# Twelve value projections moved into the first half of an attention loop, on eight cores

## The reference

```
xn  = layernorm(x)
out = x + attention(xn) + ffn(xn)
```

## Time and profile before

| | |
|---|---|
| median of 3 runs | 786.75 us (786.33 to 796.28) |
| profiled execution | 791.31 us, span of its slowest core 789.8 us |
| spans of the cores | 770.2 to 789.8 us |
| TensorE busy | 697.0 us (88%) |
| VectorE, ScalarE busy | 376.4 us (48%), 287.2 us (36%) |
| DMA queue of POOL, queue of SP | 73.08 MB and 49.77 MB |

### The profile page before, as it was taken

One profiled execution on the slowest core, in us unless ns is written; L12 is line 12 of the kernel. 1 busy time (PEld: TensorE's weight loads), 2 busy tenths in 40 slices (PEclk: granted clock), 3 DMA queues, 4 the chain that ended last, 5 costly groups with the idle time before them and its releaser, 6 DMA issues.

```text
span 789.8 us, 11732 instructions; the slowest of 8 cores (770.2 to 789.8 us)
## 1 busy us (share of the span) xinstructions
PE 697.0 (88%) x4028; PEld 333.7 (42%) x4028; DVE 376.4 (48%) x658; ACT 287.2 (36%) x437; POOL 72.0 (9%) x111
## 2 busy tenths in 40 slices
PE   1667787396999998799999997999999999999998
PEld 1233343254545444344444443444444444444443
DVE  6597876268666667631132115552464443200341
ACT  2255575489676544215564553333200000000000
POOL 2001022011101100001111111010010000000000
PEclk9999999799999999999999999999999999999999
DMA  6668487959796945626656665352265454100552
GB/s 176 121 153 179 88 154 110 207 152 264 193 271 217 247 126 165 182 109 204 187 194 213 209 218 196 124 164 103 74 198 162 146 178 131 47 0 1 160 174 66
DMA packets 70329, 123.61 MB, mean 157 GB/s; under 512 B 34176, under 2 KB 39168, under 8 KB 70272
## 3 DMA queue, kind: packets, MB, share of 16 engines
q0 software_dynamic: 22880, 73.08, 32.3%
q1 hardware_dynamic: 47392, 49.77, 23.6%
HBM read 103.30 MB, written 16.78 MB: 152 GB/s over the span
## 4 chain that ended last, share of the span: by engine, by line
PE 69%; DMA 12%; issue 7%; DVE 5%; ACT 4%; SPq 2%; POOL 0%; DVEq 0%; ACTq 0%; POOLq 0%
PE pW L947 8%; PE pY L1042 7%; PE pST L1042 7%; PE pW L1042 7%; PE pSS L1042 7%; PE pSS L1019 6%; PE pST L1019 6%; PE pY L1019 5%; PE pW L1019 5%; DMA stg<-w1r 5%; PE pW L836 4%; PE pW L824 3%; DMA stg<-w2r 3%; DMA wv_sb<-wv 2%; ACT qf L735 2%
## 5 line engine op out<-in xcount | busy, mean ns | idle before, releaser
L753 ACT ACTIVATE stg<-stg 128x2048 f32<-128x2048 f32 x32 | 60.9, 1902 | 54.2 <-DMA stg<-w2r 44.8
L590 DVE TENSOR_SCALAR w1t<-stg,consts 128x2048 bf16<-128x2048 f32 x16 | 20.5, 1283 | 115.4 <-DMA stg<-w1r 95.8
L836 PE MATMUL pW<-wv_sb,xnT 128*128 128x512 bf16 x256 | 64.1, 396 | 5.0 <-DMA wv_sb<-wv 5.0
L1042 PE MATMUL pY<-w2t,hT 128*128 128x512 bf16 x256 | 66.0, 379 | 0.7 <-DVE osb L709 0.7
L1042 PE MATMUL pST<-w2t,hT 128*128 128x512 bf16 x256 | 66.1, 379 | 0.1
L1042 PE MATMUL pW<-w2t,hT 128*128 128x512 bf16 x256 | 66.1, 379 | 0.0
L1042 PE MATMUL pSS<-w2t,hT 128*128 128x512 bf16 x256 | 66.0, 379 | 0.0
L947 PE MATMUL pW<-wo_sb,yT 128*128 128x512 bf16 x256 | 60.4, 391 | 5.0 <-ACT qf L735 3.9
L1019 PE MATMUL pSS<-xnT,w1t 128*128 128x512 bf16 x272 | 61.5, 379 | 1.7 <-ACT hT L803 1.7
L1019 PE MATMUL pST<-xnT,w1t 128*128 128x512 bf16 x272 | 61.5, 379 | 0.0
L774 ACT ACTIVATE Am<-pSS,consts 128x1024 bf16<-128x1024 f32 x32 | 35.3, 1103 | 60.2 <-PE pSS L884 60.0
(11 more groups left out here) (140 smaller groups left out, 961.6 us busy)
## 6 DMA issues: line engine op xcount, KB each, us to landing
stg<-w1r POOLq DMA_DIRECT2D x32, 1024.0 KB, 7.2
stg<-w2r POOLq DMA_DIRECT2D x32, 1024.0 KB, 6.2
xr<-x SPq DMA_DIRECT2D x16, 512.0 KB, 5.1
xre<-x SPq DMA_DIRECT2D x16, 512.0 KB, 6.6
res_scr<-rst SPq DMA_DIRECT2D x16, 512.0 KB, 3.9
res<-res_scr SPq DMA_DIRECT2D x32, 256.0 KB, 4.1
out<-osb SPq DMA_DIRECT2D x32, 256.0 KB, 2.6
wv_sb<-wv POOLq DMA_DIRECT2D x2, 1024.0 KB, 15.9
```

The costliest lines, as they stand in the source:

```text
L590: e.tensor_single_scalar(dst, src, cc(col + 1), ALU.is_lt).then_inc(sTA, 1)
L753: e.activation(buf, buf, AF.Abs, accum_out=cc(col)).then_inc(done, 1)
L836: mm = e.matmul(work_bank(u), xnT[:, c, kd, :], wv[:, hf, kd, :], start=(kd == 0), stop=(kd == KD - 1))
L1042: return e.matmul(out_bank(n), hT[:, j, 128 * t:128 * t + 128], w2t[8 * dh + j // 4][:, j % 4, :], start=(j == 0), stop=(j == NJ - 1))
```

## The change

1. **Values early.** Values of chunks 16 to 27 are projected in i = 4 to 15 (`early_v(i)` = i+12), between the two halves of `spread_q`, emptied by ScalarE into a new tile `v2` at that place in its list, and no longer projected in i = 15 to 26. i = 27 to 30 still project theirs.
2. **Queries and keys in two steps.** `proj_qk("q")` stays at the end of i % 4 == 2; `proj_qk("k")` follows `scores` of i % 4 == 3, and VectorE empties it after the mask of that iteration.
3. **Weights earlier.** The second `wv` half is issued when 6 token tiles are normalised, ahead of the block copies of queries; `wo` (before: in the middle of the loop), `b2bc` and a1 0, a1 1 follow the first block copy. SP holds back the fifth token tile until the first `wv` has landed. `A1_SLOTS` are i = 8 to 23, `TH_SLOT` is 26.
4. **Ternary pieces.** t1 0 is made in halves at the ends of i = 28 and 29, t1 1 at i = 30 and 31, t1 2 after the loop, behind the last two `empty_wo`. t2 14 gets another place in SBUF and is made with t2 15 between the two halves of the output.
5. **Rows at the end.** `empty_wo` only copies; x is not read again in the loop. Each of the 32 output pieces reads its part of x (`xs`) beside `res`, and VectorE adds it in a further instruction (`dRX`).

```diff
+def early_v(i):
+    return i + 12 if 4 <= i < 16 else None
+def has_v(n):
+    return n < 16 or n >= 28
...
-Q_BEFORE = {("a1", 2): 3, ("a1", 6): 4, ("a1", 10): 5, ("a1", 14): 6, ("t1", 2): 7}
+Q_BEFORE = {("a1", 2): 2, ("a1", 4): 3, ("a1", 8): 4, ("a1", 12): 5, ("t1", 0): 6,
+            ("t1", 2): 7}
-A1_SLOTS = list(range(10, 26))
+A1_SLOTS = list(range(8, 24))
...
+            if t == 0:
+                e.wait_ge(dV[0], 16)
             if t + 4 < NT:
                 x_in(t + 4)
...
+            if n >= 2:
+                e.wait_ge(dRX, n - 1)
+            dXS.inc(e.dma_start(out=xs[:, n % 2, :],
+                                in_=x_d[t * 128:(t + 1) * 128,
+                                        dh * 512:(dh + 1) * 512]), n)
...
+        e.wait_ge(sXN, 6)
+        e.dma_start(out=wv[:, 1, :, :],
+                    in_=wv_d[1].rearrange("k p f -> p k f")).then_inc(dV[1], 16)
         q_block(e, 1, range(4, 8), dQP)
         e.dma_start(out=wqk[:, 1, :, :], in_=wqk_d[1]).then_inc(dQK[1], 16)
-        q_block(e, 2, range(4, 8), dQP)
-        e.dma_start(out=wv[:, 1, :, :], in_=wv_d[1].rearrange("k p f -> p k f")).then_inc(dV[1], 16)
+        e.dma_start(out=wo[:].rearrange("p k (h f) -> p (k h) f", h=2, f=512),
+                    in_=wo_d.rearrange("k h p f -> p (k h) f")).then_inc(dWO, 16)
...
-                e.tensor_tensor(rst[:, c % 2, sl], work_bank(UID[key]),
-                                xre[:, c % 2, sl], ALU.add).then_inc(dW, 1)
+                e.tensor_copy(rst[:, c % 2, dh * 512:dh * 512 + 512],
+                              work_bank(UID[key])).then_inc(dW, 1)
...
-            if i == 29:
-                ternary1(0)
-            if i == 30:
-                ternary1(1)
-            if i == 31:
-                ternary1(2)
+            if i in (28, 29):
+                ternary1(0, slice(1024 * (i - 28), 1024 * (i - 27)))
+            if i in (30, 31):
+                ternary1(1, slice(1024 * (i - 30), 1024 * (i - 29)))
...
+            dXS.wait_done(e, n)
+            e.wait_ge(dRB, n + 1)
+            e.tensor_tensor(res[:, n % 2, :], res[:, n % 2, :], xs[:, n % 2, :],
+                            ALU.add).then_inc(dRX, 1)
...
             scores(i)
+            if i % 4 == 3 and i // 4 < 7:
+                proj_qk("k", i // 4 + 1)
             if more:
-                proj_v(i + 1)
+                if has_v(i + 1):
+                    proj_v(i + 1)
                 spread_k(i + 1)
             y_before(i)
             if more:
                 spread_q(i + 1, 0)
+            if early_v(i) is not None:
+                proj_v(early_v(i))
             y_within(i)
```

More of the change, by code:

```diff
@@ L268, in ln_tiles, with values @@
         return ()
+    def values(n):
+        return v2[:, n - 16, :] if 16 <= n < 28 else v[:, n % 2, :]
     def q_block(e, B, heads, done):
@@ L355, in sync_stream @@
             dRS.wait_done(e, c)
+        e.wait_ge(pH, 2 * NJ)
         res_in(0)
@@ L585, in vec_stream, with ternary @@
         tern = [0]
-        def ternary(dst, key, col, done):
+        def ternary(dst, key, col, done, part=slice(0, 2048)):
             load_done(e, key)
-            src = stg[:, STG[LID[key]], :]
+            src = stg[:, STG[LID[key]], part]
+            dst = dst[:, part]
             e.tensor_single_scalar(dst, src, cc(col + 1), ALU.is_lt).then_inc(sTA, 1)
@@ L592, in ternary, with ternary1 @@
             e.wait_ge(sTA, tern[0])
-            e.scalar_tensor_tensor(dst, src, cc(col), dst, ALU.is_gt,
-                                   ALU.subtract).then_inc(done, 1)
-        def ternary1(u):
+            last = e.scalar_tensor_tensor(dst, src, cc(col), dst, ALU.is_gt,
+                                          ALU.subtract)
+            if part.stop == 2048:
+                last.then_inc(done, 1)
+        def ternary1(u, part=slice(0, 2048)):
             if u >= 3:
@@ L630, in vec_stream @@
                             ALU.mult).then_inc(dMK, 1)
+            if i % 4 == 3 and B < 7:
+                empty_qk("k", B + 1)
             for t in ln_tiles(i):
@@ L681, in vec_stream @@
         empty_wo(31)
-        for u in range(3, 12):
+        for u in range(2, 12):
             ternary1(u)
@@ L694, in vec_stream @@
         ternary1(15)
-        for u in range(3, 15):
+        for u in range(3, 14):
             ternary2(u)
@@ L724, in empty_v @@
             unit_filled(e, ("v", i))
-            e.copy(v[:, i % 2, :], work_bank(UID[("v", i)])).then_inc(aW, 1)
+            e.copy(values(i), work_bank(UID[("v", i)])).then_inc(aW, 1)
         def empty_kx(i):
@@ L784, in sca_stream @@
                 features_q(i + 1, 0)
+                if early_v(i) is not None:
+                    empty_v(early_v(i))
                 features_q(i + 1, 1)
@@ L896, in y_before @@
             unit_emptied(e, UID[("v", i)])
-            e.matmul(yb, tril05[:], v[:, b, :], start=True, stop=False,
+            e.matmul(yb, tril05[:], values(i), start=True, stop=False,
                      skip_group_check=True)
@@ L918, in y_within @@
                 mm = e.matmul(yb[:, E * h:E * h + E], Am[:, b, h, :],
-                              v[:, b, E * h:E * h + E], start=False, stop=True,
+                              values(i)[:, E * h:E * h + E], start=False, stop=True,
                               skip_group_check=True)
@@ L929, in update @@
                          kf0[:, b, h, :, :].rearrange("p o i -> p (o i)"),
-                         v[:, b, E * h:E * h + E], start=(first and h == 0),
+                         values(i)[:, E * h:E * h + E], start=(first and h == 0),
                          stop=True, skip_group_check=True)
```

58 lines of the change are left out of this document (25 added, 33 removed).

## The result

The changed kernel takes 808.1 us (median of 4 runs, 803.4 to 810.0), the kernel before on the same chip 789.4 (4 runs, 786.3 to 796.3): a ratio of the means of 1.0216, with a 95% interval of 1.0129 to 1.0303. So it is slower; whether by more than 2% these runs don't decide. I had forecast 776.0 us and a range of 757 to 792. The time lies above both, on the far side of rival 3's price of 800 to 805. That it lies near that price is partly chance: rival 3 charges everything to iterations 3 to 8, and the table shows three stretches that missed.

A forecast was written before the change was run, and what follows sets the result against it. VectorE had most work in iterations 0 to 7, ScalarE led in 8 to 17, and TensorE was the bound from 191 to 287 us. Terms summed to -10.7 us, taking 786.75 to 776.0 us; range 757 to 792.

The forecast's parts named there:

- rival 3: Iterations 3 to 8: transposes at 6 us beside the bulk, each iteration 12 us; +30 instead of +6, 800 us; chance 0.12.
- The bulk, +6: Iterations 0 to 7: 4864 KB loading beside the transposes costs about one iteration, +6 us, bounds 0 and 30.
- Iterations 8 to 17, -3.6: ScalarE-bound stretch: early values add 1.95 us an iteration, earlier wo removes a delay; 82.1 instead of 85.7 us.
- Iterations 18 to 27, -5.6: Late iterations without the moved value projections: 90.8 instead of 96.4 us, limited by the wait for the mask.
- The plain iteration: Iterations 20, 21, 24 and 25: each shrinks by 0.73 us, from 8.63 to 7.90 us.
- the price of the queries: Iterations 18, 22 and 26: a query projection adds 1.73 us.
- The end of the loop: Iterations 28 to 31, up to the first up-projection: half ternary pieces cut 40.8 us to 33.7, -7.1 us.
- The second wv and the keys: Early iterations: second wv load beside transposes +3 us, key projection behind the scores -0.7; together +2.3.
- The up-projection and the output: After the loop: late a2 load in one staging buffer +3 us, output -0.7 us.
- rival 4: Output stage late: a pair of pieces at 8.5 us, +6 in all, 782 us; chance 0.12.
- The threshold wait: TensorE's wait for the threshold of W2: about 7 us as a sign of being right, 4.18 us before.
- The start, -5.0: First value projection: holding back token tiles removes the 4.96 us wait for wv, -5.0 us, at worst 0.

The follow-up runs named there:

- experiment 1: Changed kernel with wo, b2 and the first two W1 pieces issued behind iteration 6's block copy: Am 3 to 8 39.9 us against 52.3, mean span 787.5.
- experiment 2: Changed kernel with all values projected in their own iteration again: Am 8 to 18 73.1 us, Am 3 to 8 49.9, mean span 783.0.
- experiment 9: Changed kernel with late, spread weight loads and later second wv, without early values: 784.5 us, ratio 0.9914 to the kernel before; 782.3 us with them.
- experiment 7: Changed kernel with early values at the iteration's end, one key-spreading matmul issued four times in iterations 16 to 27: Am 18 to 28 94.4 us, mean span 783.8.
- experiment 5: Changed kernel with weight loads late and early values at the iteration's end, then also second wv later: mean spans 777.8 and 777.7 us, ratios 0.9934 and 0.9868.

## Why the prediction was wrong, step by step

- **The bulk, +6: it measured +12.4** (experiment 1; the stretch as a whole +15.5). The step that failed is the one where I took one iteration's loss "because VectorE's lead of two chunks covers the first part". The transposes slowed as the rows' maximum had shown and more (9.88 us), the lead was used up, and the projection of block 2's queries at the end of iteration 6 waited for the last of its tiles on every core. I should have worked out that due time: some 4.9 MB start before it, and with 2.8 MB that projection does not wait. Rival 3 had the mechanism, with its condition met by two pairs (10.0 and 15.0 us). Its price of +30 was too high; less than half of it came.

The kernel before already had such a place, and I passed it by. Behind the block copy of iteration 6 it starts 3328 KB:

```profile
101.92 1.55 POOL L405 DMA_DIRECT2D stg<-w1r  x2
...
105.81 6.15 SPq L287 DMA_TRANSPOSE xnT<-xn_tm  x1
112.11 6.06 SPq L303 DMA_TRANSPOSE yT<-ytm  x1
...
117.36 0.69 DVE L557 TENSOR_TENSOR ytm<-pY,consts 128x512 bf16<-128x512 f32 x1 [2.24 <-DMA yT<-ytm]
```

Its iteration 10 takes 12.8 us as a mean; in the change without early values, where no such load stands ahead of it, it takes 6.9.

- **Early values in iterations 4 to 7: I had no term for them.** They cost 2.4 us (experiment 2); three of them cost 2.8 in experiment 9.
- **Iterations 8 to 17, -3.6: they measured +5.9.** Two sizes were off. The eight early values of that stretch cost 18.0 us, not 8 x 1.95 = 15.6, since at the lower clock ScalarE waits 3.00 us for them instead of 1.48. And what is left without them was 73.1 us, not some 67: iterations with keys took 8.6 and 8.9 where I had 7.9, 8 took 8.2 and 14 took 7.8 where I had 6.6, and 16 and 17 took 6.6 each (6.4 and 6.5 in the change), where I had 6.0. The wait behind wo was named in the right place and its end was right.
- **Iterations 18 to 27, -5.6: they measured -1.5.** The plain iteration was right to 0.03 us (7.87, forecast 7.90), and so was the reader of the mask. The step that failed is the price of the queries, taken at the full clock, 1.73 us, because the earlier trace rows had 1.00 there. The slow ones go with idle time that the change itself made; experiment 7 shows this for iterations 22 and 26. Sixteen projections, each 1.6 us slower, are 3.3 us a core, most of the 4.1 us missed. The rest is there at the full clock too: from `Am` to `Am` iterations 18 and 22 took 9.9 us then (9.6 forecast for both, as my 8.9 for 18 ends at the scores), and iterations with keys took 9.9 (9.65). 27 with values and keys took 10.4, as forecast.
- **Right.** The end of the loop gave 5.9 us (forecast 7.1) and took 34.7 (33.7). The second wv and the keys cost 2.5 (2.3), with luck: experiment 5 has 4 us for the load, not 3, and 2 us of gain beside it, not 0.7. The up-projection and the output cost 1.3 together (2.3), within what this stretch varies by; the last output piece does not wait for a load as rival 4 feared. The threshold wait did not grow (3.58 us, I had said 7).
- **The start, -5.0: it measured -2.2.** The first values came 3.1 us sooner (27.8 against 30.9 as a mean); I had read 4.96 on the slowest core, where they came 1.3 us later than the mean (32.20). Another 0.9 was gone by `Am` 0; I haven't followed where.
- **The range** ended at 792, though the product in the bulk's step allowed +30. I gave 0.12 to the case whose condition I could have tested on the kernel before: two transposes of 6 us, for six iterations, are more than two chunks of lead.

## What to carry to other kernels

When a load is moved earlier, add up the bytes that start ahead of each due time, not only the mean share of the engines, and ask which small transfers travel beside it. Put an added unit behind what the limiting engine already has ready: the same projections cost 18 us between two steps of ScalarE's list and 3 us at its end. And read the waits of the kernel before for loads that stand behind a large one on their queue: here one was worth 1.2% by itself.

## What the runs showed of the hardware

A transpose by DMA that takes 1.22 us to issue took up to 9.88 us while 4864 KB were loading beside it (slowest core), and up to 9.73 us beside 2816 KB, but only in the first case did TensorE wait for it. Spreading the bytes over four iterations changed nothing (52.4 against 52.3 us). The wo load took 18.3 us before, 25.2 in the change. And with less work on TensorE some of its matmuls became slower: eight 128x512 took 3.14 us instead of 1.73 after idle stretches of 1.05 and 0.81 us, at a granted clock of 0.61 over 4 us. With three spare matmuls in each iteration none of 16 did in iterations 22 and 26 (8 without them), but 5 of 8 in iteration 18.
